# Graph network on one core: TensorE expands a near unit's cells ahead of that unit's edge features

## The reference

```python
for l in range(5):
    h = _leaky(x @ W1[l] + b1[l]) @ W2[l] + b2[l]
    e = _leaky(edge_attr @ We1[l] + be1[l]) @ We2[l] + be2[l]
    msg = h[src] * e * dot_scale[l]
    agg = segment_sum(msg, dst)
    x = layer_norm(x + agg * res_w[l])
```

## Time and profile before

| | |
|---|---|
| median of 3 runs | 23402.88 us (23347.6 to 23500.51) |
| profiled execution | 23378.29 us, span 23376.2 us |
| TensorE busy, of the span | 56% (95507 matmuls) |
| VectorE busy | 49% |
| GpSimd busy | 43% |
| ScalarE busy | 23% |
| granted TensorE clock, mean | 0.738 of full |

### The profile page before, as it was taken

How to read it: one execution, slowest core, us unless ns; L and a number is a source line. 1 busy time by engine, 2 the same in 40 slices (tenths; PEclk the granted TensorE clock), 3 DMA queues, 4 the chain that set the end, 5 groups by cost and what they waited for, 6 DMA issues and landing times. The chain is left out here.

```text
span 23376.2 us, 329567 instructions
## 1 busy us (share of the span) xinstructions
PE 13148.2 (56%) x95507; PEld 11090.2 (47%) x95507; DVE 11421.0 (49%) x19693; ACT 5323.9 (23%) x10114; POOL 9959.8 (43%) x10482
## 2 busy tenths in 40 slices
PE   0344445554556666665656566656665665666465
PEld 0222224554446556554555555555555555555455
DVE  7454444446961212115555555565565556555513
ACT  0000000112433333332222222222222222222233
POOL 0455555663024343443444444444434444444343
PEclk9666665555558778777887778887887887888787
DMA  2111111111444343442222222222222222222243
GB/s 73 37 39 39 39 39 44 52 51 59 183 149 117 110 117 106 119 116 71 65 66 64 57 64 65 59 65 66 65 55 68 66 67 57 66 65 65 76 116 91
DMA packets 1284160, 1745.76 MB, mean 75 GB/s; under 512 B 576614, under 2 KB 828390, under 8 KB 1283174
## 3 DMA queue, kind: packets, MB, share of 16 engines
q1 hardware_dynamic: 960833, 1351.53, 19.4%
q0 software_dynamic: 317440, 348.12, 7.7%
q10 hardware_dynamic: 5040, 35.13, 0.4%
HBM read 1425.04 MB, written 308.76 MB: 74 GB/s over the span
## 5 line engine op out<-in xcount | busy, mean ns | idle before, releaser
L1133 POOL DMA_INDIRECT rows_buf<-feature_table,idx_buf x4960 | 4852.9, 978 | 5615.0 <-DMA idx_buf<-src_idx 4178.9
L857 POOL DMA_INDIRECT rows_buf<-feature_parts,idx_buf x2176 | 2058.3, 946 | 2864.9 <-PE banks L912 1867.9
L899 PE MATMUL banks<-sums_space,tmp 128*128 128x192 bf16 x13720 | 2085.4, 277 | 1586.8 <-issue 1114.1
L1268 DVE TENSOR_REDUCE early<-banks 128x256 f32<-128x768 f32 (+1 forms) x1470 | 1255.8, 854 | 3153.7 <-PE banks L1205 1626.2
L869 ACT ACTIVATE sums_space<-banks 128x384 bf16<-128x384 f32 x3920 | 1637.2, 452 | 3264.0 <-PE banks L886 2400.7
L1188 PE MATMUL banks<-rest,parts 128*128 128x512 bf16 x1355 | 627.3, 463 | 3098.5 <-DVE onehot L1285 1024.2
L886 PE MATMUL banks<-table_parts,tmp 128*128 128x192 bf16 x13720 | 2081.9, 276 | 302.1 <-DMA tmp<-one_hots 281.2
L899 PEld LDWEIGHTS banks<-sums_space,tmp 128*128 128x128 fp8e4 x13720 | 1330.0, 109 | 1852.1 <-issue 1815.3
L707 POOL DMA_INDIRECT rows_buf<-attention_table,idx_buf x1664 | 1574.4, 946 | 1430.4 <-DVE parts L1447 875.1
L1180 PE MATMUL banks<-attr_buf,params 128*128 128x256 f32 x5420 | 1710.1, 443 | 670.1 <-ACT hidden L1145 435.6
L1192 PEld LDWEIGHTS banks<-params,hidden 128*128 128x128 f32 x10840 | 1910.2, 249 | 92.7 <-issue 16.4
(11 more groups left out here) (380 smaller groups left out, 24033.1 us busy)
## 6 DMA issues: line engine op xcount, KB each, us to landing
tmp<-one_hots SPq DMA_DIRECT2D x1715, 448.0 KB
one_hots<-tmp SPq DMA_DIRECT2D x245, 448.0 KB
attr_buf<-attr SPq DMA_DIRECT2D x760, 128.0 KB
attr_buf<-cell_attr SPq DMA_DIRECT2D x735, 128.0 KB
rows_buf<-feature_table,idx_buf POOLq DMA_INDIRECT x4960
gathered_rows<-rows_buf SPq DMA_DIRECT2D x208, 272.0 KB
rows_buf<-gathered_rows SPq DMA_DIRECT2D x208, 272.0 KB
rows_buf<-feature_parts,idx_buf POOLq DMA_INDIRECT x2176
```

What stands on the lines that cost most here:

```text
L857: pool.indirect_dma_start(out=far_rows[:, u, t, :], out_offset=None, in_=table3, in_offset=bass.IndirectOffsetOnAxis(ap=idx_buf[:, u, t:t ...
L899: ins = pe.matmul(bank[4 + h][:, half * 3 * D:(half + 1) * 3 * D], hot_buf[:, k, j, (2 + half) * P:(3 + half) * P], cell_rows[:, q, j % 2 ...
L1133: pool.indirect_dma_start(out=edge_rows[:, u, t, :], out_offset=None, in_=table, in_offset=bass.IndirectOffsetOnAxis(ap=idx_buf[:, u, t:t ...
L1268: dve.tensor_reduce(out=cell_row[:, 4 * part:4 * part + cells, :], in_=pair_of_banks(w.ring + part).rearrange("p (j n) -> p j n", j=4)[:, ...
```

## The change

In TensorE's turn the expand of a near unit moves ahead of the edge features of the same unit. All other engines' programs are the same, instruction for instruction.

```diff
                 def turn(w, w_later, w_ahead):
                     if w_ahead:
                         hidden_layer(w_ahead)
+                    if w_later and w_later.near:
+                        expand(w_later)
                     if w_later:
                         edge_features(w_later)
-                        if w_later.near:
-                            expand(w_later)
                     if w:
                         add_up(w)
```

## The result

The changed kernel takes 22815.17 us (median of 4 runs, 22779.84 to 22831.53) against 23418.86 (23347.6 to 23500.51) for the kernel before beside it: a ratio of 0.9739, 95% interval 0.9704 to 0.9774. It is faster by 604 us where 1431 were forecast. The direction was right, and so was the wait that the move takes away; how much of it comes back elsewhere was not.

The account below looks back on a forecast made before the run. A cycle of waits bounds the hybrid passes: TensorE's signals come late beside gathers, spacing groups 16.8 us apart. Gains of 1054 and 377 us, together 1431, gave 22000 us, range 21150 to 23200.

Parts of the forecast that it names:

- Item 1: TensorE's first eight expand matmuls run while it waits for the far multiply, at no cost; uncovered, at most 2.3 us.
- Item 2: The last six expand matmuls wait for the far sum, delaying edge features 0 to 0.4 us, covered by 3.9 us.
- Item 3: VectorE's wait before the cell sums (L1268) falls from 3153.7 us to 280; largest gain 2870 us.
- Item 4: Gather groups: one pair in four (155) follows after 10.0 instead of 16.8 us, 6.8 us each, 1054 us.
- Item 5: At 110 near-after-near places and 20 last pairs of passes the wait comes off directly, 2.9 us each, 377 us.
- The loop of the gathers holds: Rival: groups stay 16.76 us apart everywhere, only 377 us gained, 23026 us (22650 to 23200); chance 22%.
- slower rival: Gather groups without a pause hold VectorE, 20 us more per such stretch; 23972 us with 100 pairs; chance 9%.
- moved wait: Rival: VectorE waits before the near multiply (L1285) for edge features instead; no change, 23400 us; chance 6%.
- All of the wait goes: Rival: the wait before the cell sums comes off in full, 2870 us, giving 20530 us; chance 7%.

Follow-up runs that it names:

- first-half kernel: Changed kernel with only the expand's first 8 matmuls ahead of the edge features, the second half behind them: 22804.51 us, 0.9754 of the kernel before.
- chip 8: The changed kernel, unaltered, run where no TensorE signals are held: 16295.76 us against 17789.41 for the kernel before, ratio 0.9163.
- add-up was ahead too: Changed kernel with TensorE's add-up also moved ahead of the edge features: 22538.38 and 22530.15 us, 0.9642 and 0.9631 of the kernel before.
- early indices: SyncE issues the next far unit's indices one turn earlier; where signals are held, 1.004 on the order before, 0.9468 and 0.9486 on the changed order.
- plain DMAs: Far rows by one plain SyncE DMA a group from fixed rows, no GpSimd gathers in the passes: order before 21030.46 us, changed order 19450.28.
- half groups: Four of each group's eight gathers made; where signals are held, order before 21316.04 us (0.9107), changed order 20030.31 us (0.8425).

## Why the prediction was right in kind and wrong in size

- **Item 1, the first half is hidden: shown.** The first-half kernel gives the whole gain of the change, and without gathers the wait is gone.
- **Item 2, the second half delays edge features by 0 to 0.4 us, covered: shown where signals are in time** (chip 8: the second half waits 0.53 us, the edge features start no later behind the multiply than before, and the near multiply's idle time is 157.1 us against 156.1). Beside held signals it is not covered: the near multiply waits 368.2 us, and 136.2 with the second half behind. That costs nothing in time only because the cell sums wait 278 us less. The Trainium skill's rule (TensorE: Matmul & The Clock Gate, "Step-by-step: what each phase is for") that matmuls stay in program order is what the trace shows, the bias matmul 0.60 us behind the start of the second half (8576.34, 8576.94).
- **Item 3, the wait before L1268 goes: shown where signals are in time** (1710.7 to 140.3 us without gathers; 147.7 on chip 8). On the kernel as it is 1771.7 stayed, where I expected under 500. I had put 280 us on waits that the late signals leave; they left 1485.9. The step fails in one point: I took the remote waits as a fixed sum of 1261.2 us, of which the move saves 3.9 us each. But the hold goes by the gathers and not by the cell sums: it ended 12.0 us behind a group's start in 15178.30 to 15190.35, 10.7 in the pair of the earlier trace rows, and 7 to 13 us behind it in 199 of the 254 waits before and in 250 of the 323 after. A VectorE that gets there earlier therefore waits for the same end, and meets it more often, 323 times instead of 254.
- **Item 4, one pair in four gets out at 6.8 us each, 1054 us: the step that was mis-sized.** 93 more groups start within 13 us, not 155, and they gain 16.2 - 11.0 = 5.2 us each against the middle class (7141 / 441 and 2086 / 189), not 6.8: 480 us in place of 1054 (all classes together give the 553). The share of "half of those at full clock, in phase" was a guess, and it left out what follows: the wait moves to L1330, L1325 and L1285 (815 us), and the group behind an early one comes late about every other time (88 of 185, of which 50 at strip ends).
- **Item 5, 377 us at 130 places without a gather behind them: mostly wrong in its premise.** Near behind near has no far unit behind it, but gathers for later groups run beside it, and signals are held all the same. In those 110 turns the idle time before L1268 fell by 360 us (681 to 321); 469 of the 681 were remote, and only 206 ended on the expand, 1.9 us a turn and not 2.9. L1325's idle time rose by 177, which leaves 183 of 319. The ends of the passes are right: behind each pass's last gather the idle time before L1268 fell from 80 to 2 us, where I had put 58, and 613 - 553 = 60 us lie outside the group distances. So item 5 gave about 240, and since the 183 are part of the 553, items 4 and 5 together gave 613 for 1431.
- **The rivals.** None came true whole. The loop of the gathers holds in 315 of 615 distances; the slower rival's payback is there too (111 long distances for 78), but those are shorter than they were (mean 21.9 for 25.5), so what they cost above a 16.2 us distance did not grow (111 x 5.7 = 633 us for 78 x 9.3 = 725): it kept groups from getting out, it did not outweigh them. Its sign came all the same: remote waits of 8 us and more before L1268, L1285, L1325 and L1330 rose from 35 (467 us) to 80 (834 us). The moved wait showed at L1285 with 212 us, and with 1140 once the add-up was ahead too. "All of the wait goes" holds on chips 8 and 15, but with 1494 us, not 2870: the part of the 3153.7 that is remote was never the expand's.
- **The loop was half a cause.** SyncE's late indices are one of two things that hold a group back, VectorE's slot is the other. With one removed the other binds (1.004); with the expand ahead, both lie close, and the early indices bring 640 us.

What stays open: why the same program has TensorE's signals held in some groups of runs and not in others, and by what means gathers hold them. The runs tie the hold to running gathers (plain DMAs and half groups take it away) and show when it ends; nothing here shows the mechanism. Nor do they show whether the signal or the end of the matmul itself is late, since the ends are modelled; TensorE's next matmuls did go out meanwhile (L1180 at 14023.90, the sums at 14026.01). It wasn't tried to split a group's gathers with pauses between them.

## What to carry to other kernels

A wait that goes is worth what the next cycle of waits lets through. Split the idle time before it by its releaser first: here only the 1626.2 us that ended on the expand were the move's to take (1580 us came out without gathers, 1494 on a chip without held signals), and the 1261.2 us of "remote" were a hold tied to something else, which is merely met sooner. When two resources gate the same loop, as the index load and the free slot here, test an edit of one in combination with the change before it is thrown away: early indices alone made the kernel 0.4% slower, on top of the change they took 2.8% off.

## What the runs showed of the hardware

- The same program took 23.3 to 23.8 ms on four chips and 17.8 ms on two, each visited once. Where it was fast, no wait is "remote", the first pass takes 1350 us instead of 1978 in the changed order, and its granted clock is 0.96 instead of 0.81. The first pass of the changed kernel on chip 8:

```profile
8090.00:9440.00 1350.00, 1039.00 (x8574) 902.84 (x8575) 1170.13 (x2096) 482.83 (x815) 1016.04 (x988) 0.96 0.37 99
```

- TensorE's completion signals reach VectorE and ScalarE late beside GpSimd's indirect gathers on the slower chips: until 12.0 and 12.9 us after a group of eight starts (15178.30 to 15190.35, 15188.27 to 15201.14), and hardly at all with groups of four (35.0 us before the cell sums over the program). All 665 remote waits in the passes of the trace before are for semaphores that TensorE's matmuls raise.
- Gathers slow down as VectorE gets busier: 978 ns on average before, 986 after, 1029 on chip 8, where single ones take 1.38 us (8578.42) beside VectorE's work instead of 0.94. One instruction is always there: each of the 957 gathers over 1.1 us on chip 8 overlaps leaky (L1260, both inputs from `hidden`), and no gather beside L1285, L1288 or L1330 is that long there. The Trainium skill (SBUF — State Buffer, "Who interferes with whom") has VectorE and GpSimd exclude each other while a VectorE instruction runs in a 2-port mode; no row tells the mode of L1260, so the trace neither bears that out nor contradicts it. The effect stays far from deciding: 5% of 10.0 us a group.
